# Routed experts of a macaron block: 23 sorted blocks of 128 rows in place of all eight experts for every token

## What is computed

```python
def _L1_ffn_ref(hidden_states, gate_w, w_gate, w_up, w_down, sw_gate, sw_up, sw_down, shared_gate_w):
    E, K = (8, 2)            # I = 176 hidden units per expert, IS = 704 of the shared one
    logits = jnp.einsum('bsh,eh->bse', x, gate_w)
    probs = jax.nn.softmax(logits, axis=-1)
    top_w, top_i = jax.lax.top_k(probs, K)
    top_w = top_w / jnp.sum(top_w, axis=-1, keepdims=True)
    combine = jnp.einsum('bsk,bske->bse', top_w, jax.nn.one_hot(top_i, E, dtype=x.dtype))
    g = jnp.einsum('bsh,ehi->besi', x, w_gate)
    u = jnp.einsum('bsh,ehi->besi', x, w_up)
    expert_out = jnp.einsum('besi,eih->besh', jax.nn.silu(g) * u, w_down)
    moe_out = jnp.einsum('besh,bse->bsh', expert_out, combine)
    shared_out = (jax.nn.silu(x @ sw_gate) * (x @ sw_up)) @ sw_down
    return moe_out + shared_out * jax.nn.sigmoid(x @ shared_gate_w)
```

## Time and profile before

| | us |
|---|---|
| device time, median of 3 runs | 871.6 |
| lowest, highest | 870.42, 871.93 |
| span of the profiled execution, first to last instruction | 866.2 |
| passes (1,0), (1,1) | 353.06 to 424.0 |
| passes (2,0), (2,1), with the tiles of attention 1's first half | 424.0 to 586.5 |
| attention 1 | 586.5 to 714.5 |
| passes (3,0), (3,1), output | 714.5 to 866.2 |

### The profile page before, as it was taken

One profiled execution on the slowest core, in us unless ns is written; L12 is line 12 of the kernel. 1 busy time (PEld: TensorE's weight loads), 2 busy tenths in 40 slices (PEclk: granted clock), 3 DMA queues, 4 the chain that ended last, 5 costly groups with the idle time before them and its releaser, 6 DMA issues. The chain is left out here.

```text
span 866.2 us, 17819 instructions
## 1 busy us (share of the span) xinstructions
PE 781.8 (90%) x5879; PEld 515.4 (60%) x5879; DVE 633.8 (73%) x1245; ACT 446.3 (52%) x932; POOL 388.9 (45%) x383
## 2 busy tenths in 40 slices
PE   7899879999889999898889999996985989899996
PEld 3555447777457777555545655555864975555554
DVE  5989878878878777789985576557976967655544
ACT  3435568877668787444422333443755752233232
POOL 5544866675757665356653234431043003222232
PEclk8999989999989999999999999998996999999999
DMA  9900000000000000100000000000000000000000
GB/s 361 411 2 1 1 0 1 0 0 0 2 2 0 0 0 1 49 2 1 1 1 0 1 1 1 1 0 1 2 1 1 2 2 1 1 0 26 0 1 24
DMA packets 4403, 19.50 MB, mean 23 GB/s; under 512 B 737, under 2 KB 3041, under 8 KB 3713
## 3 DMA queue, kind: packets, MB, share of 16 engines
q1 hardware_dynamic: 3872, 18.55, 5.4%
q10 hardware_dynamic: 432, 0.15, 0.1%
q0 software_dynamic: 48, 0.14, 0.1%
HBM read 17.78 MB, written 1.05 MB: 22 GB/s over the span
## 5 line engine op out<-in xcount | busy, mean ns | idle before, releaser
L430 POOL TENSOR_TENSOR ARENA<-T,ARENA 128x512 f16<-128x512 f32 (+1 forms) x68 | 78.9, 1160 | 251.7 <-ACT ARENA L581 251.6
L1158 PE MATMUL PS<-XT,WC 128*128 128x512 f16 x792 | 182.4, 379 | 0.9 <-DVE T L889 0.9
L581 ACT ACTIVATE ARENA<-T 128x512 f16<-128x512 f32 (+1 forms) x100 | 63.0, 630 | 226.9 <-DVE T L894 173.7
L882 DVE SCALAR_TENSOR_TENSOR T<-T,PS 128x512 f32<-128x512 f32 (+1 forms) x100 | 68.4, 684 | 104.1 <-ACT T L570 101.5
L1158 PEld LDWEIGHTS PS<-XT,WC 128*128 (+1 forms) x792 | 76.9, 98 | 81.0 <-issue 1.9
L1158 PE MATMUL PS<-WC,ARENA 128*128 (+2 forms) x816 | 100.4, 273 | 13.6 <-POOL ARENA L430 13.2
L1158 PEld LDWEIGHTS PS<-WC,ARENA 128*128 128x128 f16 (+1 forms) x816 | 78.0, 98 | 41.7 <-POOL ARENA L430 17.3
L1158 PE MATMUL PS<-XT,WA 128*128 128x512 f16 x432 | 100.7, 381 | 0.0
L478 POOL TENSOR_TENSOR ARENA<-ARENA,ST 128x512 f32<-128x512 f32 x64 | 66.6, 1040 | 64.1 <-DVE ST L961 64.1
L570 ACT ACTIVATE T<-PS 128x512 f32<-128x512 f32 (+1 forms) x100 | 59.3, 593 | 47.1 <-PE PS L1158 47.0
L1158 PE MATMUL PS<-WA,ARENA 128*128 (+2 forms) x960 | 68.8, 212 | 12.6 <-DVE ARENA L902 11.5
(11 more groups left out here) (133 smaller groups left out, 1466.7 us busy)
## 6 DMA issues: line engine op xcount, KB each, us to landing
WB<-wb_dram SPq DMA_DIRECT2D x1, 4096.0 KB, 22.4
WC<-wc_dram SPq DMA_DIRECT2D x1, 3456.0 KB, 38.0
WC<-wc_dram SPq DMA_DIRECT2D x1, 3072.0 KB, 30.3
WA<-wa_dram SPq DMA_DIRECT2D x4, 512.0 KB, 7.4
WA<-wa_dram SPq DMA_DIRECT2D x1, 2048.0 KB, 13.7
X<-x_dram SPq DMA_DIRECT2D x2, 512.0 KB, 6.1
WB<-wd_dram SPq DMA_DIRECT2D x1, 1024.0 KB, 4.7
out_dram<-X SPq DMA_DIRECT2D x4, 256.0 KB, 2.2
```

Of the source, the lines that this page charges most:

```text
L430: pl.tensor_tensor(HH[r, a, 1, :], T3[r, :], HH[r, a, 0, :], ALU.subtract).then_inc(hid_lo, 1)
L581: sc.activation(HH[r, a, 0, :], T3[r, :], ACT.Copy).then_inc(hid_hi, 1)
L882: v.scalar_tensor_tensor(T2[r, 0, :], T1[r, 0, :], 1.0, PS[r, GATE[a], :], ALU.add, ALU.mult).then_inc(gated, 1)
L1158: ins = te.matmul(dst, left(a), right(b), start=first and n == 0, stop=last and n == 2, skip_group_check=True)
```

## The change

Passes f = 2 and 3 keep the shared expert alone: `JS` = 6 tiles in place of 17 for each half, all unrolled, without `SEL` and the third product; the shared gate is applied when the result is added to `X` (`add_shared`). The routed experts go another way.

**Routing.** `routing_ranks` also makes a mask of chosen experts; `prefix` on TensorE counts, by a product with a triangle of ones, each token's place among the tokens of its expert; `routing_slots` turns this into two row numbers per token (`IDX`, expert times 1024 plus place) and, for the second half, into a table `TBL` of 23 blocks (`NBK`): each block's expert and its first row.

**Scatter.** GpSimd writes the normed tokens, `XN`, to those rows of the table `xs_rows` in device memory (9216 rows of 256), by 8 indirect DMAs of 128 rows for each half.

**Blocks.** For each of 23 blocks SyncE reads the first row from `TBL` into a register and loads 128 rows; TensorE turns them, makes gate and up of the block's expert in one bank (6 matmuls of 352 columns, weights by a register read from `TBL`), turns the 176 hidden units as two pieces of 88, and makes the output (6 matmuls of 256 columns); ScalarE and VectorE do the splits and the activation; SyncE stores 128 rows to `ys_rows`. The work of a block is spread over three iterations.

**Gather.** When all blocks are stored, GpSimd issues 16 indirect DMAs that fetch each token's two rows, and `combine` on VectorE adds them with their weights.

**Around it.** The blocks stand behind the second of the six steps of the second half (`PRE` = 2). Attention 1's first half is prepared on its own, after the norm of phase 4, and no longer inside pass (2,1). `WD` is split inside the first blocks. The experts' weights come in as `WE` (18 DMAs) early and `WN` (26 DMAs) where `WD` alone came; both tables in device memory are zeroed at the start (9.4 MB each). `up` alternates between two banks in all passes.

```diff
--- before.py
+++ after.py
+JS = 6
+NBK = 2 * TOK // P + E - 1
+PRE = 2
...
+            for c, i0, n, part, at in pieces(KH):
+                e, k = part // 2, part % 2
+                sp.dma_start(WN[at:at + n, (e + 1) * N_N + k * D:(e + 1) * N_N + (k + 1) * D],
+                             wc_in[i0:i0 + n, c * C_N + 2 * D:(c + 1) * C_N]).then_inc(dma_n, 16)
             sp.dma_start(WD[:, D_N:], wd_in).then_inc(dma_d, 16)
+            def expert_blocks(m):
+                sp.wait_ge(table_done, m + 1)
+                for hf in range(2):
+                    sp.wait_ge(scattered[hf], 16 * 2 * TPH * (m + 1))
+                def load(b):
+                    at[b] = sp.value_load(TBL[0:1, 1, b:b + 1], min_val=0, max_val=ROWS // P - 1)
+                    after(sp, xb_turned, g - 2)
+                    sp.dma_start(XB[:, g % 3, :], XS[ds(at[b] * P, P), :]).then_inc(xb_in[g % 3], 16)
+                def store(b):
+                    sp.wait_ge(ye_copied, g + 1)
+                    sp.dma_start(YS[ds(at[b] * P, P), :], YB[:, g % 3, :]).then_inc(yb_out[g % 3], 16)
+                for b in range(NBK + 6):
+                    if b < NBK:
+                        load(b)
+                    if b >= 6:
+                        store(b - 6)
...
+            def scatter(n, hf):
+                pool.wait_ge(dma_z, 32)
+                pool.wait_ge(idx_done, ROUTED.index((n, hf)) + 1)
+                for t in range(TPH * hf, TPH * hf + TPH):
+                    for k in range(2):
+                        pl.indirect_dma_start(XS, bass.IndirectOffsetOnAxis(ap=IDX[:, k, t:t + 1], axis=0),
+                                              XN[:, t // 2, t % 2, :], None,
+                                              bounds_check=ROWS - 1).then_inc(scattered[hf], 16)
...
+            def expert_blocks(m):
+                for i in range(NBK + 2):
+                    if i < NBK:
+                        gate_tanh(i)
+                    if i >= 2:
+                        result(i - 2)
+                    if i + 2 < NBK:
+                        tokens_high(i + 2)
+                    if 1 <= i <= NBK:
+                        hidden_high(i - 1)
+                    if m == 0 and 2 <= i < 10:
+                        split(*split_d(i - 2))
...
+                for i in range(NBK + 2):
+                    if i < NBK:
+                        hidden(i)
+                    if i + 2 < NBK:
+                        tokens_low(i + 2)
+                    if 1 <= i <= NBK:
+                        hidden_low(i - 1)
...
+                for i in range(NBK + 2):
+                    if i < NBK:
+                        gate_up(i)
+                    if i >= 2:
+                        project(i - 2)
+                    if i + 2 < NBK:
+                        turn_tokens(i + 2)
+                    if 1 <= i <= NBK:
+                        turn_hidden(i - 1)
...
-            glu(2, 1, left_down(2, 0))
+            glu(2, 1, left_down(2, 0), (0, PRE))
+            expert_blocks(0)
+            glu(2, 1, nothing, (PRE, JS))
+            turn(4, 0)
+            last_down(2, 1)
             attention1()
             glu(3, 0, nothing)
-            glu(3, 1, left_down(3, 0))
+            glu(3, 1, left_down(3, 0), (0, PRE))
+            expert_blocks(1)
+            glu(3, 1, nothing, (PRE, JS))
             last_down(3, 1)
```

678 lines of the change are left out of this document (475 added, 203 removed).

## The result

| | before | after |
|---|---|---|
| device time, median (5 runs each, side by side), us | 870.42 | 882.79 |
| lowest, highest | 870.03, 871.93 | 878.71, 887.51 |
| ratio, 95% interval | | 1.0145 [1.0121, 1.0169] |
| span of the profiled execution | 866.2 | 885.7 |

The forecast was 865.4 and faster. The profiled execution of the changed kernel is the slowest of its five runs. I read details in the first profile and judge sizes by the second.

A forecast was written before the change was run, and what follows sets the result against it. TensorE was taken to bound the kernel, with a chain through four engines and device memory replacing removed work. 0.5 + 4.5 + 2.5 - 13.7 = -6.2 from 866.2 gives 860.0, plus 5.4 is 865.4 us; range 846 to 912, likeliest case 850 to 885.

The forecast's parts named there:

- Price of a block: Each of 46 routed blocks takes 2.5 us; TensorE's own work of 1.99 is the lower bound.
- the ring: In the blocks, copies, low part, projection and handovers that wait on each other across iterations: some 2.4 us per block.
- The rival of register loads: Register loads on TensorE's queue bound the blocks at 3.3 us each, 37 us more: 902 us; chance 0.14.
- Price of an indirect DMA: Each scatter or gather costs GpSimd 1.2 us, nearer a fixed cost than one by rows; a scatter lands in 2.5.
- The dear rival: Scatters and gathers at 2.0 us each: 38 us more plus some 6 of hold-up, 909; decides from 1.33; chance 0.17.
- (1,0) and (1,1), +0.5: ScalarE waits about 2 us for the 26 `WN` loads, VectorE loses splits: together +0.5 us (-1.5 to +4).
- (2,0) to the first scores, +4.5: First mixture: first block at 51 us, blocks to 106, gathers to 132, scores at 167 against 162.5 before.
- Attention 1, +2.5: First half's start: added results +3.8 us, a lost wait -1.9, routing +0.5.
- (3,0) to the end, -13.7: Second mixture: first block at 50 us, blocks to 105, end at 138 against 151.7 before.
- The signs named: Expected in the profile: TensorE idle 8 to 9 us before first block, 13 before tiles; scores at 591, pass (3,0) near 722.
- the rival of half clock: TensorE runs the blocks at 1.2 GHz, period some 4.0 us, 69 us more: 934 us; chance 0.05.
- The first 350 us: Start of the kernel, where 18.9 MB of zeros are written beside weight loads: no loss expected, one would prove the forecast wrong.

The follow-up runs named there:

- the second: Second profile: the changed kernel itself, unedited, run again on another chip; 882.18 us, ratio 1.0141 to the kernel before, profiled span 880.8.
- experiment 4: Changed kernel with the hidden rows' high and low parts made first in ScalarE's and VectorE's order of a block; 886.15 us, ratio 1.0183.
- experiment 7: Changed kernel with scatters and gathers of each token's second expert carrying 64 rows, not 128; 883.08 us, one run.
- experiment 5: Changed kernel with the expert output weights in two packed loads, issued earlier, before attention's last projections; 877.95 us, ratio 1.0084.
- the second experiment's kernel: Changed kernel with the first eight scatters issued two at a time behind pass (2,0)'s first four low parts; 887.99 us, on another chip 878.56.
- Experiments 2 and 3: 2: the second experiment's kernel. 3: changed kernel with four of eight second scatters ahead of the last low part, both mixtures; 878.44 us, ratio 1.0087.

## Why the prediction was wrong

**What bounds the kernel, and what is removed: right.** TensorE's busy time fell, and the chain through four engines and device memory became the bound of both mixtures.

**Price of a block: right, and for the reason given.** Forecast 2.5, measured 2.47; experiment 4 shortened the ring by two copies and the period went to 2.30. The ring as summed was 2.4; the 0.1 on top, for the register load, was a guess that met the number. The rival of register loads (3.3) is out. The 22 periods took 53.7 and 53.0, forecast 55. The Trainium skill, "DMA: Bandwidth & Descriptors", section "Latency and other measured facts", has the floor of such a load at about 600 ns, by which TensorE's side would be an estimated 2.6. Experiment 4 has 2.30 with the load in place, so at least part of the load runs under other work.

**Price of an indirect DMA: nearly right.** Forecast 1.2; measured 1.28 for scatters and 1.36 on average for gathers, so 16 + 8 of them cost some 3 us more per mixture than in the sum, against a threshold of 1.33. That it is a fixed cost was argued from SyncE's issues and is shown by experiment 7. The dear rival at 2.0 did not come. But one of its reasons, that VectorE would act on these transfers too, has the traces for it. In the twelve profiles other than that of experiment 7, 510 of them began, behind another one, while VectorE was idle or inside an operation that reads PSUM or has a single input, and none took more than 0.99 (scatters) or 1.03 us (gathers). 155 began while VectorE was inside an operation with both tensor inputs in SBUF; 111 of these took longer, up to 1.94. No run removes such an operation, so this is a count and not an experiment. The effect is small: 0.9 of the 21.7 us of the first mixture's gathers. The Trainium skill's rule of "SBUF — State Buffer", section "SBUF: two separate sides", is about two-port operations, and no run here tries such an operation against an indirect DMA by itself, so it stays untested.

**(1,0) and (1,1), +0.5: the step that failed first.** The landing was right: "landed at 367.7" is 14.6 us behind the stage's start, and it took 13.2. The step that failed is the other side of the wait: ScalarE's "third tile, whose gate is ready, by two steps of 3.90, the hosted turns and half a step, near 365.5". That is 12.4 us behind the stage's start, and the tile was ready at 6.5, as in the kernel before at 6.4: the first tile's gate is made inside attention's last steps, ahead of the border from which the steps were counted, and the hosted turns come behind the third gate. So the wait is 6.66 and not 2. It cost 5 us (experiment 5), and some 2.5 more stay in the pass without it, of which the sum had next to nothing.

**(2,0) to the first scores, +4.5: three terms.** "Begun, I estimate, 3 us ahead of 424.0, they cost nearly nothing": the scatters began 0.1 ahead of the stage; the text itself said that they would hold up the low part if they were late, and they did, by 4.79 us and a stretch at half clock. "GpSimd ends its last low part near 32.5": it ended at 38.0, and the scatters stand behind it. Of these 5.5 us, 2.7 are the first scatters' doing (the logits come at 23.9, forecast 21.2; 21.4 in the second experiment's kernel), 1 is a slower table, and the rest is the way from the table through the last tile's products and high part, 3.3 us for 1.5. So the first gate came at 56.4 and not at 51. Experiments 2 and 3, which move the scatters and nothing else, took 2.6 and 6.5 of this back: that shows both causes. The third is the way from the last gate to the scores, 66.0 in place of 61: gathers 21.7 in place of 19.2, begun 10.1 us after the last gate and not 6.7. No run tries the two by themselves.

**Attention 1, +2.5: right** (+3.1). **(3,0) to the end, -13.7: right in kind** (-11.2): its first block came at 49.1, forecast 50, the blocks took 53.0 for 55, but the way out 38.4 for 33: the pipeline empties at 2.13 per block, the last store lands in 3.38, each gather is dearer. The signs named are off by the same amounts: TensorE idles 7.1 and 9.2 us ahead of the first blocks (8 to 9) and 10.9 ahead of the tiles (13), the first scores come at 609.2 (591), pass (3,0) at 740.3 (722).

**Slips in the forecast's own arithmetic.** At 2.9 us per indirect DMA its terms give 953 with the hold of 6 us that it has for 2.0, and 961 with the hold that they give for 2.9 itself, not 955. Of the range 850 to 885, 57% lie below 869.9 and not two thirds, which makes the chance of faster 0.43 and not 0.47. Neither changes the forecast.

**The clock.** I expected a full clock in the blocks, and between the first and the last gate of either mixture it was 0.99, so the rival of half clock is out. Outside them, waits of some microseconds were often followed by matmuls at half clock. Pass (2,1) shows it behind a wait of 2.59 us, and pass (3,1) has the same wait and no fall behind it:

```profile
471.47 4.39 PE L1458 MATMUL PS<-XT,WC 128*128 128x512 f16 x12 [2.59 <-DVE T L1135]
771.08 2.75 PE L1458 MATMUL PS<-XT,WC 128*128 128x512 f16 x12 [2.59 <-DVE T L1135]
```

The first of the two cost nothing, since TensorE had 7.08 us to wait for the first block behind it; those behind the waits of 4.79 and 6.00 did. The sum had nothing for this in any stage; between (2,0) and the scores the granted clock is 0.87, and was 1.00 before. The Trainium skill, "TensorE: Matmul & The Clock Gate", section "Part 1: The HAM clock gate", has the throttled state as the default, which activity releases; that side of the sentence, the fall with each new idle stretch, the forecast left unused. The first of the two rows bears it out, and the second shows that a wait of that length doesn't always bring it.

**The first 350 us**, named as a place to be wrong, cost 1.8 us by the second profile. At 75 us, while the zeros are being written, TensorE is 0.4 us late in the first profile. Where the rest arises wasn't tried.

The blocks and the first block of the second mixture came a little better than forecast, by 1 to 2 us each. The sum took nearly every new wait at its best: the larger misses are waits of 2 to 7 us, all of one sign, and the gain forecast, 6 us, was smaller than two of them together.

## What to carry to other kernels

Where a change takes work from the bounding engine and puts a chain in its place, list each queue in which a link of the chain stands behind something else, and price each with the state in which the stage really begins; a gain smaller than two such waits is no forecast of a gain. A wait has two ends: the time at which the instruction would be ready without it is to be read from its row in the trace before, not counted from a stage border. And order decides here more than amount: with the same work, moving instructions within their queues, and one load forward that the host had packed, took 27 us off the kernel and made it 1.7% faster than the one before, while two edits that looked as good in one queue closed a ring through the others and cost 4 and 16 us.

## What the runs showed of the hardware

- An indirect DMA occupies GpSimd for 0.97 (scatter) to 1.01 us (gather) at 128 rows of 1 KB and 0.91 to 0.95 at 64, with 0.30 to the next; how many rows it moves hardly matters. Begun while VectorE was inside an operation with both tensor inputs in SBUF, 111 of 155 took longer, up to 1.94; of 510 others, none.
- 1.4 MB onto 88 partitions had landed 13.4 us after the first of 26 issues, which alone took 11.6, and 13.1 us after a single issue with a load of 1 MB beside it. The 1 MB landed in 14.8 there, and in 4.8 and 5.1 without the other (changed kernel, experiment 5).
- Storing 128 rows of 1 KB landed in 1.7 us in the median and in 3.38 for the last, on which the gathers wait.
- TensorE's clock fell to half behind waits of 2.5 to 6 us, but not behind each: the same wait of 2.59 us has a fall behind it in pass (2,1) and none in (3,1).
- On one of the three chips of the experiments every profile of a kernel with the blocks has a stop of 4 us, always at the same place. The kernel before, which has no profile there, took its usual time (869.9).
